# A last graph layer whose turned input is built by accumulating transfers instead of transposes

## The reference

```python
h = maximum(layernorm(x), 0)
h = relu(adj @ (h @ Wg0 + bg0))            # per batch
h = relu(adj @ (h @ Wg1 + bg1))
for p in 1..4:                             # LSTM over windows of p rows; its last state
    h[:, p-1::p, :] = lstm_p(windows of h) # replaces the window's last row
x = x + h
h = maximum(layernorm(x), 0)
v0, v1, v2 = h @ W[0], h @ W[1], h @ W[2]
x = x + diag(adj) * v0 + triu(adj, 1) @ v1 + tril(adj, -1) @ v2 + bias
```

## Time and profile before

| | us |
|---|---|
| median of 3 runs | 401.44 (401.22 to 401.57) |
| span of the profiled execution | 399.1 |
| TensorE busy | 393.3 |
| VectorE busy | 346.5 |
| ScalarE busy | 287.4 |
| GpSimd busy | 44.0 |
| group 0 with the start | 0 to 105 |
| group 1, units and the join behind | 105 to 199.6 |
| group 2 | 199.6 to 295 |
| group 3, units | 295 to 374 |
| tail | 374 to 399 |

### The profile page before, as it was taken

The page is one execution under the profiler, slowest core; times in us unless marked ns, Lnnn a source line. Parts: engine busy times, 40 slices in busy tenths (PEclk is TensorE's granted clock), DMA queues, the critical chain, the costliest instruction groups (busy, mean ns, idle before and its releaser), DMA issues.

```text
span 399.1 us, 6598 instructions
## 1 busy us (share of the span) xinstructions
PE 393.3 (99%) x2394; PEld 345.3 (87%) x2394; DVE 346.5 (87%) x886; ACT 287.4 (72%) x579; POOL 44.0 (11%) x44
## 2 busy tenths in 40 slices
PE   8999999999999999999999999999999999999997
PEld 7787889998987789899877879899797788989886
DVE  6569999998998998887998898988898979787897
ACT  4668777875897777777689676777589677767554
POOL 4910200100300003000110000300020000000250
PEclk9999999999999999999999999999999999999999
DMA  7830000000000000000000000000000000000003
GB/s 205 315 140 2 0 0 2 2 0 2 0 1 2 26 28 0 28 2 1 2 16 10 28 0 29 0 28 1 2 2 26 0 28 26 2 26 3 0 0 133
DMA packets 5503, 11.18 MB, mean 28 GB/s; under 512 B 1120, under 2 KB 2528, under 8 KB 4960
## 3 DMA queue, kind: packets, MB, share of 16 engines
q1 hardware_dynamic: 5472, 10.77, 7.5%
HBM read 6.57 MB, written 4.19 MB: 27 GB/s over the span
## 4 chain that ended last, share of the span: by engine, by line
PE 79%; DVE 14%; ACT 4%; issue 1%; DMA 1%; POOL 0%; SPq 0%; DVEq 0%; ACTq 0%
PE PS L549 11%; PE PS L540 11%; PE PS L541 10%; PE PS L572 6%; PE PS L569 6%; PE PS L568 6%; PE PS L615 5%; PE PS L490 4%; PE PS L480 4%; PE PS L472 4%; PE PS L457 3%; PE PS L607 3%; PE PS L608 3%; PE PS L609 3%; ACT GT L869 2%; PE PS L582 1%
## 5 line engine op out<-in xcount | busy, mean ns | idle before, releaser
L869 ACT ACTIVATE GT<-PS,BG 128x256 f32<-128x256 f32 (+2 forms) x312 | 157.9, 563 | 17.5 <-PE PS L572 12.8
L540 PE MATMUL PS<-HH,WIH 128*128 128x256 f32 (+2 forms) x312 | 107.2, 344 | 0.1
L541 PE MATMUL PS<-HH,WIL 128*128 128x256 f32 (+2 forms) x312 | 102.7, 330 | 0.0
L549 PE MATMUL PS<-HL,WIH 128*128 128x256 f32 (+2 forms) x294 | 97.3, 331 | 0.6
L884 ACT ACTIVATE TC<-CS 128x512 f32<-128x512 f32 (+2 forms) x88 | 44.9, 510 | 43.6 <-DVE CS L1014 32.5
L387 POOL TENSOR_TENSOR RS<-VE,NHALF 128x4 f32<-128x4 f32 (+2 forms) x18 | 29.9, 1661 | 344.5 <-DVE VE L950 263.9
L540 PEld LDWEIGHTS PS<-HH,WIH 128*128 128x128 f32 x312 | 58.8, 188 | 9.3 <-DVE HH L1052 4.3
L541 PEld LDWEIGHTS PS<-HH,WIL 128*128 128x128 f32 x312 | 58.9, 189 | 3.9 <-issue 1.2
L549 PEld LDWEIGHTS PS<-HL,WIH 128*128 128x128 f32 x294 | 55.5, 189 | 6.6 <-DVE HL L1060 2.4
L572 PE MATMUL PS<-SL,WHH 128*128 128x256 f32 (+2 forms) x192 | 60.1, 313 | 0.2
L568 PE MATMUL PS<-SH,WHH 128*128 128x256 f32 (+2 forms) x192 | 59.9, 312 | 0.0
(11 more groups left out here) (95 smaller groups left out, 655.5 us busy)
## 6 DMA issues: line engine op xcount, KB each, us to landing
out_tbd<-X SPq DMA_DIRECT2D x15, 256.0 KB, 2.0
X<-x_tbd SPq DMA_DIRECT2D x3, 1024.0 KB, 12.9
WI<-wih_t SPq DMA_DIRECT2D x1, 1024.0 KB, 5.2
X<-x_tbd SPq DMA_DIRECT2D x3, 256.0 KB, 3.7
WH<-whh_t SPq DMA_DIRECT2D x1, 768.0 KB, 6.6
X<-x_tbd SPq DMA_DIRECT2D x2, 128.0 KB, 2.4
WL<-w_l SPq DMA_DIRECT2D x1, 192.0 KB, 6.4
WG<-wg SPq DMA_DIRECT2D x2, 64.0 KB, 2.8
```

Of the source, the lines that this page charges most:

```text
L540: pe.matmul(dst, WIH[:, p - 1, cols], x_high, start=True, stop=False)
L541: pe.matmul(dst, WIL[:, p - 1, cols], x_high, start=False, stop=False)
L549: mm = pe.matmul(dst, WIH[:, p - 1, cols], x_low, start=False, stop=(j == 0))
L869: act.activation(GT[:, s, q, 0:n], bank(s, q)[:, 0:n], ACT.Tanh if q == C else ACT.Sigmoid, bias=BG[:, 4 * (p - 1) + q:4 * (p - 1) + q + 1 ...
```

## The change

For the groups 0 to 2 the turned input isn't transposed any more. The host passes x a second time, turned (x_dbt: features on the partitions, and within a group in the order pair, t, batch of the pair, which is HF's). SyncE loads 1 MB of it into H3 per group. GpSimd then issues transfers that add to what lies in H3: HF, 512 KB for each stream, and minus the mean, which SyncE first writes to a small tensor in HBM (MEANS, in 8-byte pieces) and GpSimd broadcasts over all 128 partitions, again 512 KB for each stream. H3 then holds the centred, turned x; ScalarE makes HTH from it with relu (`turn_up`) and VectorE HTL. The two batches of a pair lie interleaved, so `last_value` reads HTH and HTL with a step of two elements.

The bias is added to the group's X by one more accumulating transfer of GpSimd, 1 MB in 512-byte pieces, once all statistics are taken. VectorE has a new wait before it overwrites HF in units 0 and 1. TURN, CENTRE, SHIFT and `centre_up` are gone in these groups, HTH has places of its own (TURN_AT), and VALUE 8 to 15 move to earlier units. The last group's own last layer is as before.

```diff
-START = {(1, 1): (Piece(TURN, 0, 1, None),), (1, 3): (Piece(SUM, -1, 0, None),),
-         (2, 2): (Piece(VALUE, 0, 1, (TURN, 0)),), (3, 0): (Piece(VALUE, 1, 0, (SUM, -1)),),
+START = {(1, 3): (Piece(SUM, -1, 0, None),),
+         (2, 2): (Piece(VALUE, 0, 1, None),), (3, 0): (Piece(VALUE, 1, 0, (SUM, -1)),),
...
-         (4, 1): (Piece(TURN, 1, 1, (VALUE, 2)),), (4, 3): (Piece(SUM, 0, 0, (VALUE, 3)),),
-         (5, 1): (Piece(VALUE, 4, 1, (TURN, 1)),), (6, 1): (Piece(VALUE, 5, 1, (VALUE, 4)),),
+         (4, 3): (Piece(SUM, 0, 0, (VALUE, 3)),),
+         (5, 1): (Piece(VALUE, 4, 1, (VALUE, 2)),), (6, 1): (Piece(VALUE, 5, 1, (VALUE, 4)),),
...
-         (8, 0): (Piece(TURN, 2, 0, (VALUE, 7)),), (8, 3): (Piece(SUM, 1, 1, (FORGET, 7)),),
-         (9, 3): (Piece(VALUE, 8, 0, (TURN, 2)),), (10, 3): (Piece(VALUE, 9, 1, (SUM, 1)),),
-         (11, 3): (Piece(VALUE, 10, 0, (FORGET, 10)),), (12, 3): (Piece(VALUE, 11, 1, (FORGET, 11)),),
-         (13, 3): (Piece(TURN, 3, 0, (FORGET, 12)),), (14, 3): (Piece(SUM, 2, 1, (FORGET, 13)),)}
+         (8, 0): (Piece(VALUE, 8, 0, (VALUE, 7)),), (8, 3): (Piece(SUM, 1, 1, (FORGET, 7)),),
+         (9, 3): (Piece(VALUE, 9, 0, (VALUE, 8)),), (10, 3): (Piece(VALUE, 10, 1, (SUM, 1)),),
+         (11, 3): (Piece(VALUE, 11, 0, (FORGET, 10)),), (14, 3): (Piece(SUM, 2, 1, (FORGET, 13)),)}
+TURN_AT = {(1, 1): 0, (4, 1): 1, (6, 0): 2, (10, 0): 3}
...
-START_LATE = {4: ((OWN, 0),), 5: ((CENTRE, 2), (SHIFT, 0)), 6: ((SHIFT, 1), (SHIFT, 2))}
+START_LATE = {4: ((OWN, 0),), 5: ((LOW, 2),), 9: ((LOW, 3),)}
...
-    at={**START, (15, 1): (Piece(VALUE, 12, 0, (TURN, 3)),), (16, 3): (Piece(VALUE, 13, 1, (SUM, 2)),),
-        (17, 3): (Piece(VALUE, 14, 0, (FORGET, 16)),), (18, 3): (Piece(VALUE, 15, 1, (FORGET, 17)),)},
+    at={**START, (12, 3): (Piece(VALUE, 12, 1, (FORGET, 11)),), (13, 3): (Piece(VALUE, 13, 0, (FORGET, 12)),),
+        (15, 1): (Piece(VALUE, 14, 0, (VALUE, 13)),), (16, 3): (Piece(VALUE, 15, 1, (SUM, 2)),)},
...
+            def load_turned(g):
+
+                if g > 0:
+                    sp.wait_ge(turn_low, QUADS * g)
+                sp.dma_start(H3[:, :, :].rearrange("p b t -> p (b t)"), x_dbt[:, g, :]).then_inc(xt_in, 16)
+
+            def spread_means(g, s):
+
+                n = STREAMS * g + s
+                sp.wait_ge(var2, 2 * n + 1)
+                sp.dma_start(MEANS[g, s, :].rearrange("(c t e) -> t c e", c=HB // 2, e=2),
+                             MINUS2[:, s * HB:(s + 1) * HB].rearrange("t (c e) -> t c e", e=2)).then_inc(means_out[s], 16)
...
+            load_turned(0)
+            for i in range(GROUPS - 1):
+                for s in range(STREAMS):
+                    spread_means(i, s)
+                if i > 0:
+                    store(i - 1, (LAST,))
+                store(i, range(LAST))
+                if i < GROUPS - 2:
+                    load_turned(i + 1)
...
+                pool.wait_ge(xt_in, 16 * (i + 1))
                 for s in range(STREAMS):
+                    pool.wait_ge(lstm_step, STEPS * i + STEPS_BEFORE[LAST_OF[s] + 1])
+                    pool.dma_start(turned_stream(s), HF[:, s, :, :, :].rearrange("p c t e -> p (c t e)"),
+                                   accum_op=ALU.add).then_inc(xt_summed[s], 16)
+                for s in range(STREAMS):
+                    pool.wait_ge(xt_summed[s], 16 * (i + 1))
+                    pool.wait_ge(means_out[s], 16 * (i + 1))
+                    pool.dma_start(turned_stream(s), MEANS[i, s, :].rearrange("(a n) -> a n", a=1).broadcast_to(
+                        [128, HB * T]), accum_op=ALU.add).then_inc(xt_centred[s], 16)
                     if i > 0:
...
                     rstd(VE2, var2, 2 * STREAMS * i + 2 * s + 2, RS2, rs2, HB * s, HB * s + HB)
+                pool.wait_ge(bn2, G * (i + 1))
+                part = slice(i * G, (i + 1) * G)
+                pool.dma_start(X[:, part, :], bias.rearrange("(a c n) -> a c n", a=1, c=1).broadcast_to([T, G, D]),
+                               accum_op=ALU.add).then_inc(bias_in, 16)
...
-                high, low = (h[:, q % 2, b * T:b * T + T] for h in (HTH, HTL))
+                high, low = (of_batch(h[:, q % 2, :], g, b) for h in (HTH, HTL))
...
-                act.wait_ge(turn_mm, QUADS * g + q + 1)
+                if g == GROUPS - 1:
+                    act.wait_ge(turn_mm, q + 1)
+                else:
+                    act.wait_ge(xt_centred[q // HBANKS], 16 * (g + 1))
                 act.activation(HTH[:, q % 2, :], ps, ACT.Relu).then_inc(turn_high, 1)
...
-                for q in range(ON_SCALAR):
-                    centre_up(i, q)
...
+                if i > 0 and last_unit(k, s) is None:
+
+                    dve.wait_ge(xt_summed[s], 16 * i)
...
+                else:
+                    dve.wait_ge(bias_in, 16 * ((QUADS * g + q) // QUADS + 1))
```

More of the change, by code:

```diff
@@ L109 @@
-START_LATE = {4: ((OWN, 0),), 5: ((CENTRE, 2), (SHIFT, 0)), 6: ((SHIFT, 1), (SHIFT, 2))}
+START_MID = {0: ((OWN, -1),), 4: ((LOW, 1),), 5: ((ADD, 0),), 7: ((OWN, 1),), 9: ((ADD, 1),), 12: ((OWN, 2),)}
+START_LATE = {4: ((OWN, 0),), 5: ((LOW, 2),), 9: ((LOW, 3),)}
 STEADY = Plan(
-    at={**START, (15, 1): (Piece(VALUE, 12, 0, (TURN, 3)),), (16, 3): (Piece(VALUE, 13, 1, (SUM, 2)),),
-        (17, 3): (Piece(VALUE, 14, 0, (FORGET, 16)),), (18, 3): (Piece(VALUE, 15, 1, (FORGET, 17)),)},
-    f_after={**START_F, 16: (VALUE, 12), 17: (VALUE, 13), 18: (VALUE, 14), 19: (VALUE, 15)},
-    quads=QUADS, between=START_BETWEEN, mid=START_MID, late={**START_LATE, 9: ((CENTRE, 3), (SHIFT, 3))})
@@ L117 @@
-LATE = Plan(at=START, f_after={**START_F, 16: (TURN, 3), 17: (SUM, 2)}, quads=LAST,
-            between=START_BETWEEN, mid=START_MID, late={**START_LATE, 9: ((CENTRE, 3), (SHIFT, 3))})
+    at={**START, (12, 3): (Piece(VALUE, 12, 1, (FORGET, 11)),), (13, 3): (Piece(VALUE, 13, 0, (FORGET, 12)),),
+        (15, 1): (Piece(VALUE, 14, 0, (VALUE, 13)),), (16, 3): (Piece(VALUE, 15, 1, (SUM, 2)),)},
+    f_after={**START_F, 13: (VALUE, 12), 16: (VALUE, 14), 17: (VALUE, 15)},
+    quads=QUADS, between=START_BETWEEN, mid=START_MID, late=START_LATE)
@@ L119 @@
+LATE = Plan(at=START, f_after={**START_F, 17: (SUM, 2)}, quads=LAST,
+            between=START_BETWEEN, mid=START_MID, late=START_LATE)
 PLANS = (None,) + (GROUPS - 2) * (STEADY,) + (LATE,)
@@ L275, in program @@
         pool_shifted = sem("pool_shifted")
-        turned_up = sem("turned_up")
         centred = sem("centred")
+        xt_in = sem("xt_in")
+        xt_summed = [sem(f"xt_summed{s}") for s in range(STREAMS)]
+        xt_centred = [sem(f"xt_centred{s}") for s in range(STREAMS)]
+        means_out = [sem(f"means_out{s}") for s in range(STREAMS)]
+        bias_in = sem("bias_in")
         turn_mm = sem("turn_mm")
@@ L355, in _, with store @@
                 sp.dma_start(X[:, g * G:(g + 1) * G, :], x_tbd[:, g * G:(g + 1) * G, :]).then_inc(x_rest, 16)
-            def store(i):
-                for q in range(QUADS):
+            def load_turned(g):
[7 more added lines that the diff above has]
+                             MINUS2[:, s * HB:(s + 1) * HB].rearrange("t (c e) -> t c e", e=2)).then_inc(means_out[s], 16)
+            def store(i, quads):
+                for q in quads:
                     pieces = END_PIECES if i == GROUPS - 1 and q == LAST else ((0, PACK),)
@@ L368, in store @@
                         sp.dma_start(out_tbd[:, part, :], X[:, part, :]).then_inc(stored, 16)
-            for i in range(GROUPS):
-                store(i)
+            load_turned(0)
[7 more added lines that the diff above has]
+                    load_turned(i + 1)
+            store(GROUPS - 2, (LAST,))
+            store(GROUPS - 1, range(QUADS))
             sp.wait_ge(stored, 16 * (GROUPS * QUADS + len(END_PIECES) - 1))
@@ L643, in last_piece @@
                     wait_read(after, g)
-                if what == TURN:
-                    last_turn(g, n, bank(s, F))
-                elif what == VALUE:
+                if what == VALUE:
                     last_value(g, n, bank(s, F))
@@ L814, in copy_value @@
                                scale=RS2[:, n:n + 1]).then_inc(value_sb, 1)
-            def centre_up(g, q):
-                if q == 0:
-                    act.wait_ge(var2, 2 * STREAMS * g + 1)
-                for b in range(q * PACK, (q + 1) * PACK):
-                    done = act.activation(H3[:, b, :], X[:, g * G + b, :], ACT.Relu, bias=MINUS2[:, b:b + 1])
-                done.then_inc(turned_up, 1)
             def last_copy(piece, g):
-                if piece.what == TURN:
-                    turn_up(g, piece.n, bank(piece.s, F))
-                elif piece.what == VALUE:
+                if piece.what == VALUE:
                     copy_value(g, piece.n, bank(piece.s, F))
@@ L1180, in last_step @@
                     return
-                if what == CENTRE:
-                    centre(g, q)
-                elif what == SHIFT:
-                    add_bias(g, q)
-                elif what == LOW:
```

(3 more changed lines are left out.)

48 lines of the change are left out of this document (26 added, 22 removed).

## The result

The changed kernel takes 466.45 us (median of 4 runs, 465.00 to 467.82) against 401.43 us (401.22 to 401.57) for the kernel before: a ratio of 1.162 (95% interval 1.159 to 1.165). The prediction was 396.6 us with a range up to 404.0. Its profiled execution has a span of 463.2 us against 399.1. One execution of one kernel further down, `e5_bias_long_early`, took 631.5 us at a mean granted clock of 0.56; it is left out of that kernel's median, and since it was the profiled one, no trace of that kernel is read.

The account below looks back on a forecast made before the run. The prediction took TensorE to bound the kernel: 5.3 us of turns removed, less 0.5 us charged at units 17 to 19, is 4.8 us; 401.44 - 4.8 = 396.6 us, with an 8-in-10 range of 395.4 to 404.

Parts of the forecast that it names:

- The price of the bias transfer: GpSimd's 1 MB accumulating transfer onto X: 9.3 us plus 1.0 for its issue, 10.3, within 11.9 us available; cost 0.
- The upper end: Bias transfer with three times the part growing with bytes and 3.1 us for the issue: 16.5 us, costing 1.6 a group.
- The slack at OWN 0: VectorE's first use of X with the bias: half of 6 us counted as slack, so up to 14.9 us is free.
- Rival (b): The bias comes late at OWN 0: costs from 15 us on, 20 us would give 411.9 us; chance 0.06.
- What leaves TensorE: Twelve turns of four transposes in groups 0 to 2, each holding the chain for 0.44 us: 5.3 us.
- both turns should be given back in full: Units 1 and 4: ScalarE's waits of 0.52 and 0.69 us for TensorE each cover the 0.44 us taken out.
- rival (c): Half of the 5.3 us stays on ScalarE at units 1 to 5 or VectorE at 17 to 19: 398.8 us; chance 0.15.
- The means: Write, issue and broadcast before HTH at unit 1: 8.9 us against 9.35 available in group 1 and 11.25 in group 2; cost 0.
- rival (a): The means come late at HTH and TensorE waits: at the upper end 6.1 us of stalls, 402.7 us; chance 0.22.
- Rival (d): GpSimd and VectorE hinder each other while descriptors are made: 399.6 us, or 397.8 if the issues are held up; chance 0.07.
- Strided loads: TensorE's 144 loads of HTH and HTL with a step of two elements: 0 to 1.4 us, taken as 0.
- VectorE's 12 us: VectorE loses 18 instructions of 0.68 us a group, 12 us in all; not the bound, so gain taken as 0.

Follow-up runs that it names:

- e5_bias_long_early: The changed kernel with the bias read in 8 KB rows from HBM and issued before the means of stream 1: 399.83 us, ratio 0.996 to the kernel before.
- e6_htl2_after_copy: `e5_bias_long_early` with HTH and HTL of quad 2 two places later in unit 6, behind ScalarE's copy of VALUE 5: 398.58 us, ratio 0.9929 to the kernel before.
- e1_no_bias: The changed kernel without the bias transfer and the waits on it, groups 0 to 2 computed without bias: 400.74 us, ratio 0.998 to the kernel before.
- e2_bias_vector: The changed kernel with VectorE adding the bias of groups 0 to 2 again, in units 5, 6 and 9: 400.94 us, ratio 0.999 to the kernel before.

## Why the prediction was wrong

**The price of the bias transfer** is the step that failed. It was worked out from a plain store of 256 KB and a plain load of 1 MB, that read each byte once. For the additions that price was even a little too high: with the issue HF's sums took 4.7 us and the means' 5.1, against 1.0 + 5.1 = 6.1 predicted, and in 8 KB rows this very transfer takes 8.8 against 10.3. What is different about the bias stood in the diff and was noted only as 512-byte pieces: its source is one place of 512 bytes, read 2048 times. The upper end, three times the growing part, was 16.5 us with the issue; the transfer took 32.0. The trace before has two loads with a source of this kind, 128 reads of one place each, which neither the rows nor the prediction show:

```profile
BG<-bg SPq DMA_DIRECT2D x1, 64.0 KB, 2.5
...
BIAS<-bias SPq DMA_DIRECT2D x1, 64.0 KB, 8.9
```

The second stands in the queue behind large loads, where the 0.5 KB of DIAG took 7.6 us. The 1.3 us that it took longer would be 21 us for sixteen times the reads, an estimate; BG, only 0.1 us slower than the 8 KB of BI (2.4 us), would give 1.6. So these rows don't price it, but they leave the upper end open. The means' broadcast, a row of 4 KB for each of 128 partitions, has no such trouble, nor has the bias once it is spread over sixteen places.

The Trainium skill (DMA: Bandwidth & Descriptors, "Anatomy of one DMA — SWDGE (gpsimd) path") gives 2.0 us and the bytes at 436 GB/s, an estimate of 3.2 us for 512 KB and 4.4 us for 1 MB. The traces differ: here accumulating transfers took 4.7 to 5.1 us and 8.8.

**The slack at OWN 0** was the second miss. Three microseconds, maybe six, was read from SL of unit 5, that is, from the wrong consumer. OWN 0 on VectorE holds up ADD 0 behind it, ADD 0 frees the F bank, and gate F of unit 6 takes it at once. 22.0 us of wait on VectorE gave 21.8 on TensorE: the slack is about 0.2 us. The transfer also started later than the 111.6 of the prediction, at 113.85: the write before it took 4.65 us for 2.8, and it was half a microsecond more until GpSimd issued. So at the predicted 10.3 us, issue included, the transfer would have ended at 124.2, 0.6 us behind OWN 0; in long rows it took 8.8 and landed 0.8 us before. Rival (b) had the mechanism right and a price from 14.9 us on: by it 32.0 us would have cost 17 a group, and it was 22. Its chance of 0.06 rested on an upper end of 16.5 us that no row carried.

**What leaves TensorE.** At units 17 and 18 0.81 us a group was predicted, 0.77 and 0.76 were measured, at units 12 and 13 of the last group 0.96, against 0.97 (0.88 for the two turns and 0.09): right in both places. At units 1 and 4 "both turns should be given back in full" was wrong: 0.73 of 2.64. The two gaps of ScalarE read there were real, but between them there is none, and a loop without a gap can only take what its one or two gaps hold; VectorE is in the same loop, so what ScalarE gave up in one unit VectorE asked for in the next. That is rival (c). Its 398.8 us is nearly what `e6_htl2_after_copy` gives (398.58), but partly by luck: that kernel also has HTH moved, which (c) doesn't count.

**A step left out**: where HTH stands on ScalarE. The step from the kernel before to the change was priced by durations alone (rows of both kinds "lie within 0.04 us of each other"), not by what is queued behind. At unit 6 it stood ahead of a copy that TensorE waits for; taking it behind was worth 0.3 us in each group.

**The means.** For stream 0 of group 1 SyncE's write took 3.1 us against 2.8, half a microsecond passed until GpSimd issued, and issue and broadcast took 4.9 against 1.0 + 5.1: 8.6 us against 8.9 predicted and 9.35 available. The sum was right because its errors cancel, which is luck. HTH was in time in the changed kernel and 0.6 and 1.2 us late in `e1_no_bias`. "in time, narrowly in group 1" was right, and rival (a) is real at up to 1.8 us in one trace, not 6.

**Rival (d)** did not come. The issues of the twelve transfers with 128 rows held GpSimd for 0.9 to 1.1 us, as predicted, those of the bias for 2.4 to 2.8. Of the 50 VectorE instructions beside an issue in the changed kernel, one was clearly longer (a cast of 0.88 us for 0.44), 0.7 us in all.

**Strided loads** cost nothing. Steps of last-layer matmuls stay 0.17 to 0.18 us, and the modelled durations grow by 2 ns. The second of the three matmuls, before and in `e6_htl2_after_copy`:

```profile
L608 PE MATMUL PS<-WLL,HTH 128*128 128x384 f32 x64 | 21.5, 336 | 0.0
```

```profile
L665 PE MATMUL PS<-WLL,HTH 128*128 128x384 f32 x64 | 21.6, 338 | 0.0
```

**VectorE's 12 us.** No run takes all of it back; the part that was tested, the additions of the bias, brought nothing, as said: `e2_bias_vector` against `e1_no_bias` is 0.2 us. That could have been read one step further: an edit that takes work from an engine that isn't the bound has no gain to set against even a small chance of a late transfer.

With its bias in long rows, issued early, and HTH moved, the change brings 2.8 of the 4.8 us predicted. The shares of its chain of waits:

```profile
PE 61%; DVE 26%; ACT 10%; issue 2%; DMA 1%; SPq 0%; POOL 0%; DVEq 0%; ACTq 0%
```

The chain that was 79% TensorE is 61% here, and VectorE and ScalarE hold 36%: the rest of the gain has gone to them. In order of time it shows in group 2, unit 1:

```profile
202.44 0.64 ACT TC L936
203.18 0.71 DVE HF L1101
...
207.40 0.69 DVE X L1188
208.13 0.45 PE PS L664
```

## What to carry to other kernels

Before you price a transfer by its bytes, look at both ends of it: how many pieces, and how many of them read the same place; if thousands do, write the row out a few times first. Before you call a wait covered, go through everything queued behind the waiting instruction and find the one whose result is wanted soonest; a bank that must be free counts as a result. And work taken from a saturated engine was worth no more here than the idle time of the next engine at that very place, so add up gaps unit by unit, not by the group.
